# Near-zero counts of half the rows taken as signs on ScalarE, a later start of GpSimd's gate chunks, and another order of four steps on VectorE

## The reference

```
y   = scan(a*s + (1-a)*x) @ W.T + b + depthwise_conv5(x)         # retention and taps
x1  = layernorm(x + y)
q, k, v = x1, ctx, ctx                                            # mLSTM cell, 8 heads of 64
ig, fg  = gates(q, k, v);  cs = cumsum(log_sigmoid(fg))
D   = exp(cs_t - cs_s + ig_s - rowmax)                            # causal
x2  = layernorm(x1 + norm((q@k.T/8 * D / normaliser) @ v) * scale)
st  = [mean, std, min, max, l2, mean(|x2| < 1e-6)]  per row       # router statistics
probs = softmax(gelu([x2, st] @ r1.T + r1b) @ r2.T); top 2 of 32 experts, 160 rows each
out = layernorm(x2 + experts(x2) + adapters(x2))
```

## Time and profile before

| what | value |
|---|---|
| median of 3 runs | 1672.55 us (1671.28 to 1672.86) |
| the profiled execution, whole | 1673.45 us |
| its span, first to last instruction | 1671.3 us |
| mean granted TensorE clock | 0.940 |
| busy: PE, PEld | 1475.5 us (88%), 1127.6 us (67%) |
| busy: DVE | 943.2 us (56%) |
| busy: ACT | 488.6 us (29%) |
| busy: POOL | 310.7 us (19%) |

### The profile page before, as it was taken

One profiled execution on the slowest core, in us unless ns is written; L12 is line 12 of the kernel. 1 busy time (PEld: TensorE's weight loads), 2 busy tenths in 40 slices (PEclk: granted clock), 3 DMA queues, 4 the chain that ended last, 5 costly groups with the idle time before them and its releaser, 6 DMA issues.

```text
span 1671.3 us, 29354 instructions
## 1 busy us (share of the span) xinstructions
PE 1475.5 (88%) x10911; PEld 1127.6 (67%) x10911; DVE 943.2 (56%) x2784; ACT 488.6 (29%) x1154; POOL 310.7 (19%) x400
## 2 busy tenths in 40 slices
PE   5679998998899720699999999999999999999995
PEld 3356555555556410588878888788887878878783
DVE  8667999999996989533333423324233242332454
ACT  4556566675755443010101001010010100101023
POOL 4001121121111200111212121121211212112135
PEclk9689999999999855699999999999999999999997
DMA  6203213132130261067677676776767777676796
GB/s 175 71 22 100 76 64 106 43 99 70 67 86 1 101 280 59 17 220 295 228 286 269 235 291 214 297 258 248 288 217 292 251 260 283 220 294 239 274 349 198
DMA packets 92575, 311.03 MB, mean 186 GB/s; under 512 B 42838, under 2 KB 46940, under 8 KB 83164
## 3 DMA queue, kind: packets, MB, share of 16 engines
q1 hardware_dynamic: 79260, 287.87, 47.1%
q0 software_dynamic: 13248, 22.29, 5.9%
HBM read 273.18 MB, written 36.96 MB: 186 GB/s over the span
## 4 chain that ended last, share of the span: by engine, by line
PE 69%; DVE 20%; issue 5%; ACT 3%; DMA 2%; POOL 1%; SPq 1%; DVEq 0%; POOLq 0%; ACTq 0%
PE bank L1029 36%; PE banks L1043 14%; PE bank L654 6%; PE banks L1046 4%; DVE arena L1447 3%; DVE arena L1437 2%; DVE arena L1886 2%; PE bank L656 1%; PE banks L756 1%; DMA arena<-acc_rows 1%; DVE arena L1619 1%; DVE arena L1609 1%; PE banks L737 1%; DVE arena L1487 1%; DVE arena L1468 1%
## 5 line engine op out<-in xcount | busy, mean ns | idle before, releaser
L1382 ACT ACTIVATE arena<-bank 128x160 f32<-128x160 f32 x288 | 87.1, 303 | 873.2 <-PE bank L1029 871.9
L1029 PE MATMUL bank<-keep,arena 128*128 128x160 f32 x2304 | 320.0, 299 | 1.7 <-DVE arena L2082 1.7
L1029 PE MATMUL bank<-arena 128*128 128x160 f32 x2304 | 319.2, 301 | 0.8 <-issue 0.8
L1029 PEld LDWEIGHTS bank<-keep,arena 128*128 128x128 f32 x2304 | 315.4, 189 | 5.5 <-issue 3.2
L1029 PEld LDWEIGHTS bank<-arena 128*128 128x128 f32 x2304 | 315.4, 191 | 4.2 <-issue 4.2
L2082 DVE TENSOR_TENSOR arena<-arena,bank 128x160 f32<-128x160 f32 x256 | 82.1, 321 | 404.6 <-ACT arena L1382 352.5
L1043 PE MATMUL banks<-arena 128*128 128x512 f32 x576 | 252.4, 592 | 0.0
L2271 POOL DMA_INDIRECT acc_rows<-arena,keep x64 | 102.8, 1606 | 628.8 <-DVE arena L2027 610.9
L1043 PEld LDWEIGHTS banks<-arena 128*128 128x128 f32 x576 | 107.6, 190 | 122.5 <-issue 122.5
L2025 DVE TENSOR_SCALAR arena<-banks,keep 128x512 f32<-128x512 f32 x32 | 24.0, 750 | 189.3 <-PE banks L1046 185.6
L654 PE MATMUL bank<-arena 128*128 128x512 f32 x224 | 108.0, 627 | 7.1 <-DVE arena L1447 7.1
(11 more groups left out here) (294 smaller groups left out, 1803.7 us busy)
## 6 DMA issues: line engine op xcount, KB each, us to landing
arena<-in_wup SPq DMA_DIRECT2D x32, 4096.0 KB, 12.5
arena<-in_wdn SPq DMA_DIRECT2D x32, 2048.0 KB
arena<-in_aup SPq DMA_DIRECT2D x32, 512.0 KB, 11.6
arena<-in_xT SPq DMA_DIRECT2D x32, 256.0 KB, 2.8
arena<-in_kT SPq DMA_DIRECT2D x8, 1024.0 KB, 5.6
arena<-in_v SPq DMA_DIRECT2D x32, 256.0 KB, 6.6
x_rows<-arena SPq DMA_DIRECT2D x8, 1024.0 KB, 4.5
acc_rows<-arena SPq DMA_DIRECT2D x8, 1024.0 KB, 6.8
```

The costliest lines, as they stand in the source:

```text
L1029: m = pe.matmul(u[:, g * CAP:(g + 1) * CAP], w, xeT[e.slot][:, c, :], start=(c == 0), stop=(c == C - 1))
L1382: act.activation(sg[k], Ub[k][:, 0:CAP], ACT.Silu).then_inc(up_a(f"silu{j}"), 1)
```

## The change

Four edits:

1. For batches 0 to 5, two of the four counts leave VectorE. ScalarE instead applies a steep affine function and Sign to the squares of row tiles 0 and 1 and sums the signs (`signs_of_squares`); for batches 6 and 7 it does so for all four row tiles. The count is recovered as half the sum plus a half, in a second instruction of `router_stats` that waits for the signs. In a step the signs stand on ScalarE between `gates_0(n)` and `gates_1(n)`.
2. GpSimd's gate chunks wait for `neg` (line 1581) in place of `max` (1579).
3. `weigh_values` stands ahead of `gates_f`, both ahead of the taps of chunk 2, and one of these taps stands between `gates_f` and `gates_g`, three behind.
4. The chosen experts' numbers are written straight to where they are kept; one small copy per batch goes.

```diff
+        def signed(b):
+            return TB if b.off >= NB - 2 else TB // 2
...
+            def signs_of_squares(b):
+                act.wait_ge(*n3_a.at("squares", b))
+                for tb in range(signed(b)):
+                    rows = square_rows(b, tb)
+                    m = act.activation(rows, rows, ACT.Sign, scale=-SPARSE_SCALE, bias=sparse_at,
+                                       accum_out=sums(b)[2][:, tb:tb + 1])
+                m.then_inc(n3_s("sq"), 1)
...
                 norm3_out(b)
+                signs_of_squares(p)
                 last_copies(b)
                 squares(b)
+                signs_of_squares(b)
...
                     gates_0(n)
+                if r:
+                    signs_of_squares(n - 2)
+                if a:
                     gates_1(n)
...
-                for tb in range(TB):
+                for tb in range(signed(b), TB):
                     rows = square_rows(b, tb)
                     m = dve.tensor_scalar(rows, rows, SPARSE_SQ, None, ALU.is_lt, ALU.add,
...
-                dve.tensor_scalar(st6[:, :, 5], nz, 1.0 / D, None, ALU.mult).then_inc(ro_v("stats"), 1)
+                k = signed(b)
+                if k < TB:
+                    dve.tensor_scalar(st6[:, k:, 5], nz[:, k:], 1.0 / D, None, ALU.mult)
+                dve.wait_ge(*n3_s.at("sq", b))
+                dve.tensor_scalar(st6[:, 0:k, 5], nz[:, 0:k], 0.5 / D, 0.5, ALU.mult, ALU.add).then_inc(ro_v("stats"), 1)
...
+                ex2 = tiles_of(e_all, b)
                 dve.tensor_copy(ex2, at8[:, :, 0:2])
...
-                dve.tensor_copy(tiles_of(e_all, b), ex2)
...
+                if a:
+                    weigh_values(n)
+                    gates_f(n)
                 if x1:
-                    taps(n + 1, 2)
+                    taps(n + 1, 2, (0,))
                 if a:
-                    gates_f(n)
-                    weigh_values(n)
                     gates_g(n)
+                if x1:
+                    taps(n + 1, 2, (1, 2, 3))
...
-                pool.wait_ge(*ga_v.at("max", b))
+                pool.wait_ge(*ga_v.at("neg", b))
```

More of the change, by code:

```diff
@@ L50 @@
 SPARSE_SQ = 9.99999996004197e-13
+SPARSE_SCALE = 217.0 * 2.0 ** 28
+SPARSE_AT = 0.058250490576028824
 R_AT = TB * GROW
@@ L278, in decoder_kernel @@
         at8 = room.take(TB, 8, dt=U32)
-        ex2 = room.take(TB, 2)
         oh0 = room.take(TB, NE)
@@ L282, in decoder_kernel @@
         wsum = room.take(TB)
+        sparse_at = room.take(1)
         more_w = ST[0].rearrange("p (k c) t -> p k (c t)", k=2)
@@ L365, in decoder_kernel @@
         l2_p = steps("ln2_pool", ["eps2", "rstd2", "eps3", "minus3", "rstd3", "shift3"])
-        n3_a = steps("ln3_scalar", [f"out{tb}" for tb in range(TB)] + ["sq"])
+        n3_a = steps("ln3_scalar", [f"out{tb}" for tb in range(TB)] + ["squares"])
+        n3_s = steps("signs_scalar", ["sq"])
         ro_t = steps("router_tensor", [f"x{tb}" for tb in range(TB)] + ["st", "h0", "h1", "lg"])
@@ L1109, in squares @@
                                        accum_out=sums(b)[1][:, tb:tb + 1])
-                m.then_inc(n3_a("sq"), 1)
+                m.then_inc(n3_a("squares"), 1)
+            def signs_of_squares(b):
[5 more added lines that the diff above has]
+                m.then_inc(n3_s("sq"), 1)
             def queries(b, tiles):
@@ L1414, in _ @@
             dve.memset(posh, 0.5)
+            dve.memset(sparse_at, SPARSE_AT)
             dve.memset(ones, 1.0).then_inc(cs_v("misc"), 1)
@@ L1438, in state_scan, with taps @@
                                        ALU.mult, ALU.add).then_inc(re_v(f"scan{c}"), 1)
-            def taps(b, c):
+            def taps(b, c, which=range(TAPS - 1)):
                 row = cv[b.slot][:, c, :]
                 dve.wait_ge(*re_a.at(f"cv{c}", b))
-                for i, k in enumerate(k for k in range(TAPS) if k != PAD):
+                for i in which:
+                    k = i if i < PAD else i + 1
                     if i:
@@ L1511, in head_out @@
                     dve.wait_ge(*ro_t.at(f"x{TB - 1}", b - 2))
-                    dve.wait_ge(*n3_a.at("sq", b - 2))
+                    dve.wait_ge(*n3_s.at("sq", b - 2))
                     dve.wait_ge(*ro_v.at("extr1", b - 2))
@@ L1603, in router_sparse @@
             def router_sparse(b):
-                dve.wait_ge(*n3_a.at("sq", b))
+                dve.wait_ge(*n3_a.at("squares", b))
                 dve.wait_ge(*ro_v.at("stats", b - 1))
-                for tb in range(TB):
+                for tb in range(signed(b), TB):
                     rows = square_rows(b, tb)
@@ L1610, in router_sparse @@
                                           accum_out=sums(b)[2][:, tb:tb + 1])
-                m.then_inc(ro_v("cnt"), 1)
+                if signed(b) < TB:
+                    m.then_inc(ro_v("cnt"), 1)
+                else:
+                    dve.sem_inc(ro_v("cnt"), 1)
             def router_extreme(b, k):
```

## The result

The changed kernel takes **1714.35 us** (median of 4 runs, 1713.8 to 1715.15), against 1672.7 (1671.28 to 1673.84) for the one before. The ratio is 1.025, 95% interval 1.0232 to 1.0268: slower by 41.7 us, where 36.2 were forecast. Single executions of the kernel before differ by up to 2.6 us, so a difference of about 1 us between two traces need not come from an edit. The page begins with the span; of the slices I copy VectorE's and the granted clock in tenths.

The account below looks back on a forecast made before the run. VectorE was taken to bound the batch pipeline. Terms 30.5 + 3.8 - 2.5 + 1.0 + 3.4 = 36.2 us on the profiled 1673.45 gave 1709.7, with the median 0.9 lower: 1709 us predicted, range 1698 to 1719.

Parts of the forecast that it names:

- steps 0 and 1: Pipeline steps without signs: GpSimd's later start saves 0.5 us and weighted values first 0.35 us in each.
- stall in steps 2 to 6: VectorE waits 7.2 us for ScalarE's signs, less 1.14 us of saved counts: +6.1 us a step, 30.5 us in five.
- clock in steps 2 to 6: TensorE's idle gaps change shape, one new before the scores, so its clock may drop: +1 us, 0 to +5.
- the rest of these steps: Steps 2 to 6: GpSimd's later start, weighted values first and the removed copy change nothing: 0 us.
- step 7 up to the last norm: No scans or taps; signs delay scores, gate sum and the gates' logarithm: +3.8 us, before savings of 0.5 and 0.35.
- closing stretch: After ScalarE's last norm: eight signs take 5.1 us, less the statistics copy's 1.81 us wait: +3.4 us, to 4.9.
- Rival 1: ScalarE has the signs when VectorE asks, so no wait: 1663 us, faster; chance 5 in 100.
- Nothing absorbs it: VectorE's queue in steps 2 to 6: no existing wait shrinks or grows against the 6.1 us; `gates_1` comes 4.1 us later.
- Rival 2: The 1.6 us a step of waiting at line 1454 vanish, partly absorbing the stall: 1701 us; chance 8 in 100.
- Rival 3: New gaps slow TensorE until its scores, gate sum, router and values pass VectorE: 1.8 us in five steps, 1718 us; 12 in 100.
- GpSimd: Its later start saves VectorE 0.5 us at line 1585, given back at the next scan: 0 in steps 2 to 6.
- The other signs named ahead: Expected in the changed profile: waits for signs totalling 43 us, period 73.1 us, 12 counts, some 4 us before the scores.

## Why the prediction was right, and which terms were off

The mechanism and the main term held, and the measured time lies in the range, 5 us above the 1709 that was forecast. The two large misses, the clock and step 7, both point up, and little cancels them, so the range did not hold by luck. By checkpoints in the two traces (counts of step 2 began at 162.0 and 159.3 us, those of step 7 at 495.3 and 526.0, the last norm on ScalarE at 567.5 and 604.2, the first activation of the selection at 599.6 and 640.0):

| term | forecast | measured |
|---|---|---|
| steps 0 and 1 | -1.7 | -2.7, of which -1.3 is there before any changed instruction |
| stall in steps 2 to 6 | +30.5 | 5 x 6.0 = +30.1 |
| clock in steps 2 to 6 | +1.0 | +4.7 (the wait for the last row tile) |
| the rest of these steps | 0 | -1.3; in step 3 -0.2, of which -0.1 between the scans of chunks 2 and 3 and -0.1 the copy that goes |
| step 7 up to the last norm | +3.0 | +5.9 |
| closing stretch | +3.4 | +3.7 |

- **The counts and the wait.** The forecast was a wait of 7.2 us and a scan 6.1 us late; it is 7.07 us, and in step 2 the scan moved by 6.0. Signs were taken at 1.45 us for two. From the copy's start to their end were forecast 2.11 us; it is 2.03. Moving the wait alone gave 42 us back, which shows the cause. Rival 1, that the signs are no wait, fell with the wait of 7.07 us; its sum also left out the +3.4 of the closing stretch, with which 1663 would have been 1667.
- **Nothing absorbs it.** Right for VectorE's queue: line 1595 was reached without a wait, although both matmul groups ran at 1.2 GHz and `gates_1` came 5.9 us later and not 4.1 (8.56 us from the copy's start to it, where it was 2.71). Rival 2 fell: the wait at the retention's copy grew.
- **TensorE's clock, the term that was mis-sized.** "I put +1 us in the sum (0 to +5)": it is +4.7. Behind it stands a step that was wrong, "TensorE's states come some 1.9 us earlier, into idle time ahead of the retention ... : 0". Idle time of TensorE is not free here. Edit 3 joined two short waits into one of 4 us. Behind it the first tile is slow in all five steps, where it was in three, and the five together take 29.2 us in the changed kernel where they took 23.7; alone the edit costs 7.7 us. At that copy the signs alone bring VectorE's wait down from 7.8 to 6.0 us, and with edits 2 and 3 it is 12.5; the +4.7 is what is left of both. Rival 3 saw slow matmuls too, but behind the other gap, where they did no harm except in step 7.
- **Step 7.** The gates' logarithm came 4.8 us later (forecast 3.8). Then VectorE waited 2.7 us for TensorE's values of the third pair where it had waited 1.0, which took the 0.5 us of edit 2 and 1.2 more. The weighted values first brought nothing either: from there to the states' inputs are 8.72 us in both traces, since VectorE waits for TensorE's line 718 (now 724) 0.4 us longer.
- **GpSimd.** 0.5 us won at one instruction, 0.5 us given back at the scan, as written. The blocking read from the earlier trace rows shows in both directions; counting the 0.5 us eight times would have been wrong.
- **Steps 0 and 1.** From the gates' cumulative sum to the states' inputs on VectorE, edits 2 and 3 saved 0.68 and 0.63 us, where 0.85 each was forecast. Another 1.3 us of the difference is there at the first retention copy, before any changed instruction, and is no effect of the change.
- **The closing stretch.** The total fits, but not the way to it. The statistics copy came 5.4 us later and not 3.4 (to 4.9), since the forecast said that it would have no wait, and it has 1.46 us; some 1.6 us were won back between it and the selection.
- **The other signs named ahead** came: 42.4 us of waiting (43), a period of 73.4 us on average (73.1), 12 counts, 3.99 us ahead of the scores (4), 0.68 us at line 1585's successor, and GpSimd's second chunk at 1.29 us where it took 1.15.

## What to carry to other kernels

Moving work to an idle engine moves a wait with it: look at where in its own queue the consumer asks for the result, and what stands behind that, before counting what was saved; here the same signs cost 38 us or gained 5, by the place of one instruction of 0.17 us. Where an engine's clock falls when it idles, two short waits can be cheaper than one long one, so letting that engine finish sooner ahead of a fixed start can cost more than it brings. Matmuls that fill such a gap cost their full time wherever the gap is missing. An engine freed of a lock shifts the collision to the next instruction that needs the pair; follow both sides one instruction further.

## What the runs showed of the hardware

- In the kernel before, an idle stretch of TensorE of 1.7 us, 2.3 to 3.8 us of work and a second stretch of 0.4 to 1.9 us left a first retention tile of 3.70 us in two of five steps and of 5.4 to 5.5 in three. One stretch of 4.0 us left 6.3 to 6.4 us with edit 3 alone, and 5.2 to 6.8 with edits 2 to 4. Twelve matmuls whose result nobody reads brought it to 3.70 us in all five. Behind the same second stretch of 1.89 us the tile takes 5.40 us in one step of the kernel before and 3.70 in another; what decides between them was not found.
- ScalarE's Sign over 128x512 with a pointer for its bias and a read of its sum costs 0.71 us in a row of such, a Square with such a read 0.61, an Identity with two pointers and a read 0.80. It added no table load: both kernels have 28.
- VectorE's scan and GpSimd's chunk of 8x384 don't run fully side by side: the scan of 128x512 took 1.73 instead of 1.22 us where the chunk had begun first.
